# A two-layer transformer kernel on one core: batch 0 alone is prepared ahead, the other batches and weights between the rings

## The reference

```python
x = L0_attn_x                                  # (8, 512, 256)
xn = _layernorm(x)
# 16 heads of 64, rotary embedding on q and k, causal softmax, Wo
x = x + attention(xn, Wq, Wk, Wv, Wo) + ffn_int8(xn)
#   ffn_int8: x_scale = max(|xn|) / 127 over ALL batches; round(xn / x_scale) @ weight_int8.T
#             * x_scale * weight_scale + bias
xn = _layernorm(x)
# gated attention over the 512 rows of each batch, and a receptance/key/value FFN with a shift by one row
x = x + gated(xn, compare_left, compare_right) + r * (relu(k) ** 2 @ W_v)
```

## Time and profile before

| | |
|---|---|
| median of 3 runs | 1176.16 us (1173.99 to 1178.44) |
| the profiled execution | 1175.19 us, its span 1173.4 us |
| TensorE, VectorE, ScalarE, GpSimd busy | 87%, 76%, 59%, 65% of the span |
| mean granted TensorE clock | 0.982 |
| first projection (ring -5) | 103.80 us |
| v(0), the start of ring 0 | 142.74 us |
| end of the span | 1173.4 us |

### The profile page before, as it was taken

One profiled execution on the slowest core, in us unless ns is written; L12 is line 12 of the kernel. 1 busy time (PEld: TensorE's weight loads), 2 busy tenths in 40 slices (PEclk: granted clock), 3 DMA queues, 4 the chain that ended last, 5 costly groups with the idle time before them and its releaser, 6 DMA issues.

```text
span 1173.4 us, 23304 instructions
## 1 busy us (share of the span) xinstructions
PE 1023.0 (87%) x7944; PEld 665.5 (57%) x7944; DVE 892.0 (76%) x1869; ACT 691.4 (59%) x1831; POOL 767.5 (65%) x949
## 2 busy tenths in 40 slices
PE   2004599999999999999999999999999965899988
PEld 1002266666666766766666676676667742454444
DVE  7695577776777777777777777777777637999996
ACT  1252366766666666666666666666667604766764
POOL 0081677777877777786777777687776515756762
PEclk9998999999999999999999999999999986999999
DMA  9203433342233233223323322322332000010001
GB/s 347 83 0 126 144 102 97 96 131 82 87 112 100 82 105 121 82 95 109 95 87 110 112 85 96 109 91 89 105 97 82 1 1 1 1 37 19 19 28 45
DMA packets 99700, 100.11 MB, mean 85 GB/s; under 512 B 12928, under 2 KB 94848, under 8 KB 99200
## 3 DMA queue, kind: packets, MB, share of 16 engines
q1 hardware_dynamic: 99584, 98.63, 25.8%
HBM read 56.64 MB, written 41.94 MB: 84 GB/s over the span
## 4 chain that ended last, share of the span: by engine, by line
PE 73%; DVE 18%; issue 3%; DMA 2%; ACT 2%; SPq 1%; POOL 1%; DVEq 0%; ACTq 0%; POOLq 0%
PE bank L1267 24%; PE bank L1355 13%; PE bank L1341 12%; PE bank L1370 7%; PE bank L1328 6%; PE bank L1329 5%; DVE arena L1179 3%; PE bank L1330 2%; DMA x_sb<-in_x 2%; PE bank L1517 2%; DVE nm L1149 1%; DVE arena L916 1%; DVE wmax L950 1%; DVE arena L1198 1%; DVE nm L1021 1%
## 5 line engine op out<-in xcount | busy, mean ns | idle before, releaser
L529 POOL TENSOR_SCALAR arena<-arena,rc 128x128 f32<-128x128 f32 (+3 forms) x512 | 276.0, 559 | 197.2 <-DVE rc L1029 197.2
L698 ACT ACTIVATE arena<-bank,nm 128x256 f32<-128x256 f32 (+3 forms) x512 | 268.4, 527 | 83.9 <-DVE nm L1021 73.7
L1021 DVE TENSOR_REDUCE nm<-bank 128x1 f32<-128x256 f32 (+3 forms) x512 | 229.9, 480 | 108.5 <-PE bank L1330 105.0
L1341 PE MATMUL bank<-ident,arena 128*128 128x128 f32 x1280 | 216.6, 277 | 4.8 <-DVE arena L1036 4.4
L1341 PEld LDWEIGHTS bank<-ident,arena 128*128 128x128 f32 x1280 | 143.7, 141 | 41.2 <-DVE arena L1036 20.3
L706 ACT ACTIVATE arena<-bank 128x512 f32<-128x512 f32 (+3 forms) x256 | 111.3, 435 | 79.6 <-PE bank L1341 79.4
L1329 PE MATMUL bank<-arena 128*128 128x256 f16 (+3 forms) x512 | 153.4, 300 | 0.0
L1355 PE MATMUL bank<-arena 128*64 128x512 f32 (+3 forms) x1024 | 152.0, 439 | 0.0
L1328 PE MATMUL bank<-arena 128*128 128x256 f16 (+3 forms) x512 | 147.4, 301 | 2.7 <-ACT arena L698 2.7
L1036 DVE COPY arena<-bank 128x512 f32<-128x512 f32 (+3 forms) x256 | 124.1, 485 | 23.8 <-PE bank L1341 20.0
L1355 PEld LDWEIGHTS bank<-arena 128*64 128x64 f32 x1024 | 67.8, 136 | 94.3 <-issue 71.3
(11 more groups left out here) (148 smaller groups left out, 2225.7 us busy)
## 6 DMA issues: line engine op xcount, KB each, us to landing
arena<-scr SPq DMA_DIRECT2D x320, 128.0 KB, 2.5
scr<-arena SPq DMA_DIRECT2D x256, 128.0 KB, 1.7
x_sb<-in_x SPq DMA_DIRECT2D x8, 512.0 KB, 6.5
arena<-in_weights SPq DMA_DIRECT2D x2, 2048.0 KB, 12.4
out<-x_sb SPq DMA_DIRECT2D x16, 256.0 KB, 2.2
xscr<-xsh SPq DMA_DIRECT2D x8, 256.0 KB, 2.3
xscr<-xsl SPq DMA_DIRECT2D x8, 256.0 KB, 2.2
xsh<-xscr SPq DMA_DIRECT2D x8, 256.0 KB, 3.1
```

Of the source, the lines that this page charges most:

```text
L529: last = pool.tensor_scalar(pr[slot][:, OFF[i]:OFF[i + 1]], pr[slot][:, OFF[i]:OFF[i + 1]], rc[:, slot, i:i + 1], 1.0, ALU.mult, ALU.mult)
L698: act.activation(pr[slot][:, OFF[i]:OFF[i + 1]], s_tile[i], ACT.Exp, bias=nm[:, slot, i:i + 1], accum_out=sm[:, slot, i:i + 1]).then_inc(e ...
L1021: dve.tensor_reduce(nm[:, slot, i:i + 1], s_tile[i], AX.X, ALU.max, negate=True).then_inc(max_done, 1)
L1341: last = pe.transpose(banks[5 + h][:, (i - j) * P:(i - j + 1) * P], pr[2 * par + h][:, OFF[i] + j * P:OFF[i] + (j + 1) * P], ident[:])
```

## The change

Ahead of the rings there is now only batch 0 (loaded first; statistics, a root for its four tiles, normal rows, transposes, high and low halves, which stay in SBUF) and the weights of queries and keys. Their maxima go over partitions by TensorE: a transpose of `wmax`, VectorE's maximum of the row, a diagonal matrix of it and a product with ones. The tables of cosine and sine are made by GpSimd. High and low halves of the weights are made from the unscaled weights in one instruction each, low halves by VectorE instead of GpSimd.

All else stands in the rings. VectorE's `early(n)` comes at the end of ring n; ScalarE makes the normal rows of batch n + 1 at the end of ring n (with `nbx`, minus mean times root, as bias) and the high halves of batch n in rings 1 to 7; TensorE transposes batch n in rings 1 to 7. In rings 0 to 7 ScalarE also takes two of the four copies `pt_whole` that VectorE made. The maxima of Wo, of layer 1's weights and of the rows go over partitions through DRAM (`spread_maxima`). Quantising batch 0 moves from rings 4 to 7 to the end of ring 7. In rings -5 to -1 the odd projections have a bank of their own.

```diff
-            for b in range(NB):
-                u = b % 2
-                pe.wait_ge(xn1_done, b + 1)
-                after(pe, xtl_done, KT * (b - 1))
-                for k in range(KT):
+            def columns_of_rows(b, k):
+                pe.wait_ge(xn1_done, b + 1)
+                after(pe, xtl_done, KT * (b - 1) + KT + k if b else 0)
+                dst = banks[2 + k] if b == 0 else wo
...
-            pool.wait_ge(wmax_done, NG)
-            pool.partition_all_reduce(wall[:], wmax[:], P, bass.bass_isa.ReduceOp.absmax).then_inc(wall_done, 1)
...
+            pool.wait_ge(setup_done, 1)
+            pool.wait_ge(tab_loaded, 16)
+            for g, by, dsts in ((G_Q, L ** -0.5, (cosq, sinq)), (G_K, 1.0, (cosk, sink))):
+                for a, dst in enumerate(dsts):
+                    last = pool.tensor_scalar(dst[:], tabraw[:, a], sc[:, g:g + 1], by, ALU.mult, ALU.mult)
+                last.then_inc(tab_done, 1)
...
+            def early(n):
+
+                if n == -AHEAD:
+                    pairs_low(G_K, 0)
+                    pairs_low(G_K, 1)
+                    dve.wait_ge(wv_loaded, 16)
+                    weight_maximum(slice(G_V, G_O))
+                elif n == 1 - AHEAD:
+                    weight_scale(slice(G_V, G_O), 1)
+                    bias_rows()
+                    row_sums(1)
+                elif n == 2 - AHEAD:
+                    row_maximum(0)
+                    row_sums(2)
+                elif n == 3 - AHEAD:
+                    weights_low(G_V, (wv_hi, 1), wv_lo)
+                    row_sums(3)
+                elif n == 4 - AHEAD:
+                    inverse_roots(slice(1, 4), 1)
+                elif n == 0:
+                    row_sums(4)
+                    row_sums(5)
+                elif n == 1:
+                    row_maximum(1)
+                    row_sums(6)
+                elif n == 2:
+                    row_sums(7)
+                    inverse_roots(slice(4, NB), 2)
+                    row_maximum(2)
+                elif n == 3:
+                    weight_maximum(slice(G_O, G_L))
+                    row_maximum(3)
+                elif n == 4:
+                    weight_scale(slice(G_O, G_L), 2)
+                    row_maximum(4)
+                elif n == 5:
+                    row_maximum(5)
+                elif n == 6:
+                    weights_low(G_O, (wo_hi, 1), wo_lo)
+                    row_maximum(6)
+                    row_maximum(7)
+                elif n == 9:
+                    weight_maximum(slice(G_L, NG))
+                elif n == 10:
+                    weight_scale(slice(G_L, NG), 4)
+                elif 13 <= n < 13 + NG - G_L:
+                    weights_low(G_L + n - 13, (wr_hi, n - 12), wr_lo)
...
                 dve.wait_ge(e_mm, f + 1)
-                after(dve, r1_done, f)
+                after(dve, r0_done, f)
                 dve.scalar_tensor_tensor(out=t_ec, in0=pj[:], scalar=bias, in1=c[:], op0=ALU.add, op1=ALU.mult)
+                after(dve, r1_done, f)
                 dve.scalar_tensor_tensor(out=t_es, in0=pj[:], scalar=bias, in1=z[:], op0=ALU.add, op1=ALU.mult).then_inc(te_done, 1)
...
             def ring(n):                       # ScalarE
+                if 1 <= n < NB:
+                    columns_high(n, 0)
+                if shared_copies(n):
+                    pt_whole(n, 0, 1)
...
+                later_weights(n)
+                if 0 <= n < NB - 1:
+                    normal_rows(n + 1)
...
+            def spread_maxima(turn, src, count):   # SyncE, quads 4, 5 and 7
+                for g in range(count):
+                    sp.dma_start(mscr[turn, g].unsqueeze(1), src[:, g:g + 1]).then_inc(spread_out, 16)
+                sp.wait_ge(spread_out, 16 * (1, 2, 7)[turn])
+                sp.dma_start(spread[:, 0:count]..., mscr[turn, 0:count]...partition_broadcast(P)).then_inc(spread_in, 16)
```

529 lines of the change are left out of this document (346 added, 183 removed).

## The result

The changed kernel takes 1159.9 us (median of four runs, 1157.5 to 1160.7) where the kernel before takes 1175.5 (1174.0 to 1178.4). The ratio is 0.9861, with a 95% interval from 0.9836 to 0.9885: faster by 1.4%, about 16 us, and the interval leaves out 1. The forecast was 1127 with a range from 1104 to 1147. The sign was right, and the size was wrong by 33 us.

The account below looks back on a forecast made before the run. TensorE was busy for 1023 of 1173.4 us, and only the head, waiting on VectorE and DRAM, could shrink. -83.4 + 4 + 28 + 2 = -49.4 gave a span of 1124.0, as a run 1127; range 1104 to 1147.

Parts of the forecast that it names:

- Step 1: Head up to the first projection: starts at 20.4 us instead of 103.80, -83.4 us; bounds 19 and 24.
- Step 2: Filling rings -5 to -1: 43 us instead of 38.9, +4 us; bounds 37 and 48.
- That would bring a ring to GpSimd's own four instructions: Filling rings: the odd halves' own bank would cut a ring from 7.1 to some 4.7 us, before VectorE's added work.
- the 72: Sign of error at the end of the filling rings: v(0), ring 0's first step, coming after 72 us; about 63 was expected.
- I take half: 43 us: Filling rings: half of up to 9.3 us of VectorE delay by GpSimd, added to 38.6 us.
- Step 3: Rings 0 to 7, given the work moved out of the head: +28 us, a mean ring of 15.6; floor +4.
- the ceiling of 40: Upper bound for rings 0 to 7: +40 us, with full delays by GpSimd and 1.8 us a ring.
- the 18: Rings of batch 0 were expected at 13.3 to 18 us each, ring 2 the longest.
- I take 1.1, 7.8 in all: Rings 1 to 7: TensorE's transposes and its wait for ScalarE's copy cost 1.1 us a ring, 7.8 in all.
- rival (c): Rings fed by a late VectorE leave TensorE at 1.2 GHz, 9.4 us more each; 1202 with all eight; chance 0.03.
- I count 2.0 us a ring as free and the rest as time on the path: Rings -1 to 7: VectorE's added work above 2.0 us a ring lengthens the ring, 19.2 us, plus 1 for ring 5.
- Step 4: Rings 8 to 17: late weight maxima and low halves cost +2 us, 0 to 5; maxima through DRAM cost 0.

Follow-up runs that it names:

- Experiment 2: Changed kernel with the values' maximum transpose behind ring -4's even projection and the bias products at the end of ring -3 on TensorE: 1152.9 us, ratio 0.9803.
- experiment 1: Changed kernel, except that VectorE keeps both copies that ScalarE took over in rings 0 to 7: 1146.7 us, ratio 0.9739.
- experiment 7: Changed kernel with 24 small unused TensorE products put into the wait for ScalarE's copy in rings 1, 4, 6 and 7: 1153.8 us, ratio 0.9817.
- experiment 6: Changed kernel with both copies kept on VectorE and the row maxima of batches 1 to 7 taken over one column only: 1141.7 us, ratio 0.9698.
- experiment 9: Kernel with copies, TensorE order, keys' products and last scales altered (1130.8), VectorE's two longest early pieces moved behind the next ring's first copy: 1131.2 us, ratio 0.9636.
- experiment 4: Changed kernel with the scales of the last five weight groups read back at the end of ring 11 instead of 10: 1155.3 us, ratio 0.9814.
- experiment 10: Kernel of experiment 9 with ring 11's residual ahead of the scales and ScalarE's copies ahead of its first exponential in rings 0 to 8: 1130.3 us, ratio 0.9616.

## Why the prediction was wrong

**Step 1, the first projection: right.** 21.14 us against 20.4, -82.7 against -83.4. The rows of the loads, root and products added up. Of the queries' eight low products three took 0.91 us instead of 0.47 beside GpSimd's table products, 1.3 us in all, which the forecast had only in its upper bound. That the maxima over partitions by TensorE bring nothing there was also argued from a sound row (0.45 us for GpSimd's reduction in the earlier trace rows), but no run here tried GpSimd's way in the new place.

**Step 2, rings -5 to -1: the bank right, two prices wrong.** The sentence "That would bring a ring to GpSimd's own four instructions" is supported: without the bank of its own the kernel loses 10.9 us. Against the +4 forecast stood +14.4, and v(0) came at 74.5, past the 72 that I named as the sign of being wrong. What I missed is the order on TensorE. I added up VectorE's work ring by ring, as if TensorE were always ready, and never followed what the change queued on TensorE ahead of the even projections. Experiment 2 gives 6.5 us of v(0) for that. Of the exclusion I took half ("I take half: 43 us"). For the keys' products it came nearly in full: 3.9 us lost, where I had set 4.6 for the full price and so counted 2.3. For the bias rows VectorE's four diagonal matrices lost some 2.8 of the 3.5 that I had set in full: three took 1.19 to 1.25 us beside the rotation and the last, behind it, 0.28. The values' low half wasn't held up (2.34 us); it held up GpSimd, whose product beside it took 3.25 us instead of 1.27. With the order and the keys' products put right, v(0) stands at 61.6 against the 63 forecast.

The links of the root in ring -1 behave as forecast, from 0.14 to 1.21 us. In the changed kernel, VectorE and below it GpSimd:

```profile
76.17 0.63 DVE L1003 SCALAR_TENSOR_TENSOR nw<-nw 128x12 f32<-128x12 f32 x1
76.84 1.21 DVE L999 TENSOR_TENSOR nw<-nw 128x12 f32<-128x12 f32 x1
78.08 1.19 DVE L1001 SCALAR_TENSOR_TENSOR nw<-nw 128x12 f32<-128x12 f32 x1
79.30 0.17 DVE L1003 SCALAR_TENSOR_TENSOR nw<-nw 128x12 f32<-128x12 f32 x1
```

```profile
74.74 2.05 POOL L607 TENSOR_SCALAR arena<-arena,rc 128x128 f32<-128x128 f32 x4 [2.90 <-DVE rc L1235]
76.75 1.27 POOL L579 TENSOR_TENSOR arena<-arena 128x512 f32<-128x512 f32 x1
77.98 1.26 POOL L581 TENSOR_TENSOR arena<-arena 128x512 f32<-128x512 f32 x1
```

Each GpSimd instruction lets one link through. It also holds for GpSimd's normalisation (the link of 0.63 beside its 0.51 each), which the trace of before hadn't shown. Reductions are not held up: the row maximum takes 1.21 us at 130.48, where GpSimd is idle, and 1.21 at 162.32, where it is busy throughout. The Trainium skill (SBUF — State Buffer, section Who interferes with whom) describes a lock between a VectorE instruction with two inputs in SBUF and any GpSimd instruction that reads SBUF, which spares reductions. These rows agree with it, the normalisation included.

**Step 3, rings 0 to 7: two terms failed.** +44.6 against +28, and above the ceiling of 40 (v(0) to v(8) alone, +38.9, just under it). Rings 0 and 3 take 19.1 and 21.0 us, past the 18 that I had named for the longest. The forecast was the sum of 7.8 for copies and transposes and 20.2 for all else.

The first is the term "In rings 1 to 7 TensorE also waits for a copy that ScalarE now makes behind a high half; with the transposes 0.9 to 1.8 a ring, I take 1.1, 7.8 in all". The two copies alone cost 11.0 us of it (experiment 1), with the transposes still there, and net of the 1.06 us a ring of which they relieve VectorE. I had seen the wait. What I didn't see is what a second wait right behind a first one does in these rings: the projection behind the two runs at 1.2 GHz, 1.3 us more a ring, and at full clock when either wait is gone or filled (rings 2 and 5, experiments 1 and 7). That is rival (c) in small. I had worked it out for a whole ring, given it 0.03, and left it out of the sum, although the trace of before had the price of one block on show (2.73 against 1.48 in the earlier trace rows).

The second is "I count 2.0 us a ring as free and the rest as time on the path", which gave the 20.2. With the copies back on VectorE 33.6 us are left (experiment 1). Some of the difference of 13.4 is the copies' own time on VectorE, 8.5 us busy, of which perhaps half is handed on (an estimate by experiment 6's half), and what the transposes cost, which no run separates. The rest is work that I had called free or cheap. Half is handed on even from blocks of 1.1 us (experiment 6), and the place matters little (experiment 9): the chain of experiment 1 shows a loop between VectorE and ScalarE that sets the ring, and not a slack ahead of one maximum. Half of it was missed where the copies play little part: ring 0, with the first roots ahead of it, is 6.9 us longer than before (6.1 in experiment 1) against 3.4 forecast, and ring 8, with batch 0's quantising, 5.7 (6.0) against 2.0. In rings 0 and 3 TensorE waits 4.3 and 5.1 us for ScalarE and then runs a projection at the lower clock, in experiment 1 as well.

**Step 4, the route through DRAM: wrong.** "their two landings fit into a ring of 12 us; I cost them at 0". They took 15.8 us from the first issue to VectorE and stopped it for 5.53 in ring 10, for 0.73 at the end of ring 7 and not at all in ring 4. The places of the stops were named, and their price was not: +7.1 against +2. Of this 3.2 comes back with the one-ring delay of experiment 4. The stops at the ends of rings 4 and 7 come and grow as the rings get shorter: up to 1.31 and 2.40 us in experiment 10.

Together: order on TensorE 6.5, the keys' products 6.1, the copies 11.0, the stop 3.2, so 26.8. Undone at once they give 28.2 us, and the kernel then takes 1130.8 against 1127 forecast. That it comes so near is in part luck, since the forecast was for a kernel with the copies and the stop in it. What stays open: how much of ring 8's 19 to 20 us is exclusion (the quantising steps stand beside GpSimd) beside the 0.7 to 2.4 of the stop, which wasn't tried; what the transposes of rings 1 to 7 cost; and whether ScalarE's normal rows are on the path.

## What to carry to other kernels

When work moves into a pipeline that runs in order, write down for every engine what stands behind each new wait; here a few small TensorE products and one copy, each on the engine that seemed to have time, cost 6.5 and 11 us. Price a wait of TensorE with the slow block behind it, not by its length alone. Share a copy with an idler engine only where nobody's next instruction hangs on it: of two such copies one cost time and one saved it.

## What the runs showed of the hardware

- Writing one 4-byte value a partition to DRAM took long: the next instruction of SyncE, which waits for it, came 7.9 us after the last of five such writes in the changed kernel (issues up to 247.0, next at 254.9) and 8.8 and 8.6 us after a single one (7.9 in experiment 1, 6.8 in experiment 7); reading the block back to all partitions took 4.4 to 5.1 us. How much of this is other traffic no run tells.
- TensorE that is kept busy with products nobody needs made the kernel 5 to 6 us faster: in the four rings where they filled the second of two waits (0.4 to 1.3 us, then 1.85), the six products of the next block took 1.3 us instead of 2.0 to 2.6.
- A VectorE instruction of 128x12 that takes 0.17 us alone took 1.2 beside a GpSimd product of 1.27, 128x128 ones 1.2 instead of 0.28, and three of 128x256 0.91 instead of 0.47 beside GpSimd's products for the tables.
- GpSimd took 1.2 us for a 128x256 product with two per-partition operands that are both read from SBUF, and ScalarE starts the same rows 0.49 us apart. GpSimd's product of 128x256 with one such operand takes 0.48. How much of the 1.2 is waiting for VectorE no run tells.
